# Twelve of the 832 edge steps get their node rows from SyncE, one register-addressed transfer a row, in place of GpSimd's gather

## The chip, the cores and the metric

One core of a Trainium2 chip runs the whole program. The metric is the device time of one execution in microseconds (us), as the median of several; lower is better. TensorE (PE), VectorE (DVE), ScalarE (ACT), GpSimd (POOL) and SyncE (SP) each run a program of their own and meet at semaphores. "Landed" is said of a DMA transfer when its completion has been signalled.

## The reference

A graph attention layer and a mixture of experts follow each other, each with a layer normalisation ahead and a residual around it. This change lies in the attention layer:

```python
N = 6250; E = 100000; H, F_IN, F_OUT = (8, 256, 32)
src, dst = (edge_index[0], edge_index[1])
h = jnp.einsum('ni,hio->hno', x, W)
attn_src = jnp.einsum('hno,ho->hn', h, a_src[..., 0])
attn_dst = jnp.einsum('hno,ho->hn', h, a_dst[..., 0])
edge_attn = jax.nn.leaky_relu(attn_src[:, src] + attn_dst[:, dst], negative_slope=0.2)
edge_attn_exp = jnp.exp(edge_attn - jnp.max(edge_attn))
attn_sum = jax.ops.segment_sum(edge_attn_exp.T, dst, num_segments=N)
attn_norm = edge_attn_exp / (attn_sum[dst].T + 1e-10)
out = jax.ops.segment_sum((attn_norm[..., None] * h[:, src]).transpose(1, 0, 2), dst, num_segments=N)
```

After it come a top-2 choice among 16 experts and two matrix products per expert (256 to 512 to 256), which the change does not touch.

## The kernel before, in words

The first stage normalises x, multiplies it by the weights and stores one row of 264 numbers a node (256 features, 8 attention terms; 1056 bytes) in the DRAM table `node_rows`. The edges are sorted by destination. They are cut into chunks of 128, and a chunk that crosses a border between two tiles of 128 destination nodes is worked once for each tile; that makes at most 832 steps (`STEPS`), in 104 groups of 8 (`GROUP`). The edge stage runs over the groups:

- GpSimd (`gpsimd_program`, L827) issues one indirect gather a step: 128 rows of `node_rows`, by the 128 indices of a column of `src_idx`, into `gathered[g % 4][:, j, :]`. There are four slots of eight steps. Before every second gather it waits until the matmuls of the same steps four groups earlier are done (`agg_mm`), since they read the slot.
- SyncE (`load_dloc`, L504) loads one broadcast block of local destination numbers a group, three groups ahead. It waits for the one-hot of three groups earlier (`onehot_t_ok`, from L1367). Between two of these it has nothing else to do.
- VectorE goes through a group in a fixed order, here called its turn. It sums the destination's terms (L1374), waits for the group's eight gathers and adds the sources' terms (`edge_logits_add`, L1381), then the leaky ReLU (L1386) and the maximum (L1392, L1397, L1399). Between nine or so adds of finished sums into the accumulator (`add_step`, L1419 and L1421) stand the one-hot of the next group (L1367) and four products of rows and weights (`weigh`, L1407), each over two steps. It reads the accumulator's tile numbers into registers with a register load (L444).
- ScalarE takes the running maximum (L688), writes the exponentials into the gathered rows (L693) and into PSUM (L695), and makes the one-hots for the sums.
- TensorE multiplies one-hots by weighed rows (`aggregate`, L973), two groups behind: the sums of group g - 2 stand in turn g. In the last eight turns (`CATCH_UP`) it has nine steps a turn, so that the last group is not two behind.

In the experts' stage SyncE loads an expert's first matrix for each of 113 slots, by an expert number that it reads into a register eight at a time (`experts_of`, L460) and uses as the offset of a transfer (L587). Lines are those of the kernel before.

Of the kernel before, what the change touches and what calls it, by code (L numbers as in the profile page):

```python
# [7 lines left out]
ACT = mybir.ActivationFunctionType  # L8
AXIS_FREE = mybir.AxisListType.X
F32 = mybir.dt.float32  # L10
I32 = mybir.dt.int32
# [30 lines left out]
SLOT_TILES = (NODES * TOP_K + EXPERTS * (P - 1)) // P  # L42
PAIRS = -(-TILES // 2)
Y_ROW = F_IN + TOP_K
KC = F_IN // P
# [5 lines left out]
def build_program(nc, x, src, dst, w_gnn, a_src, a_dst, gate_w, gate_b, w1, b1, w2, b2, gamma, beta, out):  # L51
    ctx = ExitStack()
    with ctx:
# [17 lines left out]
        dloc_rows = dram("dloc_rows", [STEP_BLOCKS * P, P], BF16)  # L71
        chunk_rows = dram("chunk_rows", [2 * CHUNK_PARTS * CHUNK_COLS])


# [198 lines left out]

        row_in = [sem(f"row_in{i}") for i in range(4)]
        rows_b_ok, dloc_out = sem("rows_b_ok"), sem("dloc_out")
        dloc_in = [sem(f"dloc_in{i}") for i in range(3)]
# [102 lines left out]
        slot_at.append(region1[:, fourth:fourth + GROUP * ROW])  # L379
        gathered = [v.rearrange("p (j c) -> p j c", c=ROW) for v in slot_at]  # L380
        Z_BANKS, M_BANK, AGG_BANKS = (2, 3), 4, (0, 1, 5, 6, 7)
        AGG = len(AGG_BANKS)
# [83 lines left out]
        def sync_program(d):  # L466
# [39 lines left out]
            for t in range(TILES):  # L506
# [16 lines left out]
                if t in ROWS_AT:  # L523
                    n = ROWS_AT.index(t)
                    d.wait_ge(rows_b_ok, n + 1)
                    d.dma_start(dloc_rows[n * P:(n + 1) * P, :], rows_b[:, n, :]).then_inc(dloc_out, 16)
            store_h(TILES - 1)
            d.wait_ge(dloc_out, 16 * STEP_BLOCKS)
            for g in range(3):
                load_dloc(g)  # L530


            for g in range(3, GROUPS):
                load_dloc(g)

            def store_y0(q):
# [78 lines left out]
        def scalar_program(s):  # L615
# [70 lines left out]
            for g in range(GROUPS):  # L686
                s.wait_ge(max_bc, g + 1)
                s.activation(neg_max[:, g + 1:g + 2], bank[M_BANK][:, P + 8:P + 9], ACT.Copy,  # L688
                             scale=-1.0).then_inc(neg_max_ok)
                s.wait_ge(neg_max_ok, g + 1)  # L690
                s.wait_ge(z_relu, g + 1)

                s.activation(gathered[g % SLOTS][:, :, F_IN:ROW], z[:, g % 2, :, :], ACT.Exp,  # L693
                             bias=neg_max[:, g + 1:g + 2])
                s.activation(p_bank(g), z[:, g % 2, :, :], ACT.Exp, bias=neg_max[:, g + 1:g + 2]).then_inc(p_ok)  # L695
                s.activation(fall[:, g:g + 1], neg_max[:, g:g + 1], ACT.Exp, scale=-1.0,
                             bias=neg_max[:, g + 1:g + 2]).then_inc(fall_ok)
                onehots(g)
                if g % 2 == 1 and g // 2 < TILES:
                    x_plus_xn(g // 2)  # L700
# [81 lines left out]
        def gpsimd_program(p):  # L782
# [32 lines left out]
            for g in range(GROUPS):  # L815
# [5 lines left out]
                if g == SLOTS - 1:  # L821
                    p.wait_ge(b1_col_ok, 1)
                for j in range(GROUP):
                    k = g * GROUP + j
# [71 lines left out]
        def tensor_program(pe):  # L896
# [69 lines left out]
            def aggregate(steps):  # L966
                for k in steps:
# [3 lines left out]
                    if k >= AGG:  # L971
                        pe.wait_ge(acc_add, k - AGG + 1)
                    pe.matmul(bank[AGG_BANKS[k % AGG]][:, 0:ROW], onehot[:, (g % 3) * GROUP + j, :],  # L973
                              gathered[g % SLOTS][:, j, :], start=True, stop=True).then_inc(agg_mm)
            pe.wait_ge(xnt_ok, TILES)
# [171 lines left out]
        def vector_program(v):  # L1147
# [229 lines left out]
            def edge_logits_add(g):  # L1377
                zg = z[:, g % 2, :, :]
                v.wait_ge(z_sum, g + 1)
                v.wait_ge(row_in[g % SLOTS], GROUP * landed(g, SLOTS))  # L1380
                v.tensor_tensor(zg, zg, gathered[g % SLOTS][:, :, F_IN:ROW], ALU.add).then_inc(z_add)  # L1381

# [19 lines left out]
            def weigh(g, quarter):  # L1402
                v.wait_ge(p_ok, g + 1)
                js = slice(quarter * 2, quarter * 2 + 2)
                hv = gathered[g % SLOTS][:, js, 0:F_IN].rearrange("p j (h o) -> p j h o", o=F_OUT)
# [436 lines left out]
```

## Time and profile before

| what | us |
|---|---|
| time, median of 3 runs (lowest to highest) | 1995.41 (1995.39 to 1996.13) |
| the profiled execution, first to last instruction (its span) | 1782.4 |
| median minus span | 213.0 |
| first gather of the edge stage starts | 91.5 |
| last gather starts | 1132.6 |

The profile is of one further execution, and what it gives as that execution's own time is its span; the 213.0 us between the span and the median of the runs lie outside it. The edge stage takes 1041.1 us from the first gather's start to the last one's. Busy shares over the span are 80% for PE, 62% for its weight loads (they overlap), 66% for DVE, 43% for ACT and 68% for POOL.

### The profile page before, as it was taken

How to read it: one execution, taken by the hardware profiler on the slowest of the kernel's cores; microseconds unless marked ns; L12 is line 12 of the kernel's file. 1: busy time of each engine (PE TensorE's matmuls, PEld its weight loads, DVE VectorE, ACT ScalarE, POOL GpSimd, SP SyncE). 2: the span in 40 equal slices, each digit the busy share in tenths (PEclk: the TensorE clock that was granted, in tenths of full speed). 3: DMA queues.
4: the chain of work that ended last, by engine and by line, in shares of the span. 5: the costliest groups of instructions: out<-in, count | busy, mean ns of one | idle time of the engine just before them, and what ended most of it. 6: DMA issues, size and time to landing. Idle time of an engine off the chain costs nothing.

```text
span 1782.4 us, 28293 instructions
## 1 busy us (share of the span) xinstructions
PE 1417.7 (80%) x6757; PEld 1097.9 (62%) x6757; DVE 1173.9 (66%) x3565; ACT 775.1 (43%) x2345; POOL 1206.3 (68%) x1237
## 2 busy tenths in 40 slices
PE   4937877777777878778777877667699999999965
PEld 3725555545555555455554555466599999999953
DVE  6767777777777777777777777799734443332348
ACT  2634545455454545454454544444323333333335
POOL 3077777777777777777777777337457667656747
PEclk9957677777777776876777687855599999999987
DMA  6555555545554555554444445364579778878875
GB/s 199 182 143 132 138 134 137 134 133 137 134 137 133 139 132 138 133 134 137 132 139 132 139 131 142 100 213 148 143 213 223 212 207 218 212 201 212 212 182 184
DMA packets 166544, 284.22 MB, mean 159 GB/s; under 512 B 31743, under 2 KB 93268, under 8 KB 166228
## 3 DMA queue, kind: packets, MB, share of 16 engines
q0 software_dynamic: 62256, 143.99, 32.9%
q1 hardware_dynamic: 101764, 137.90, 25.7%
q8 instruction: 65, 1.06, 0.2%
q10 hardware_dynamic: 2368, 0.52, 0.2%
q14 instruction: 91, 0.75, 0.1%
HBM read 240.97 MB, written 42.16 MB: 159 GB/s over the span
## 4 chain that ended last, share of the span: by engine, by line
PE 41%; POOL 23%; DVE 14%; issue 11%; DMA 8%; DVEq 2%; ACT 0%; ACTq 0%; POOLq 0%; SPq 0%
POOL region L827 22%; PE bank L1104 11%; PE bank L1116 11%; PE bank L973 10%; DMA region<-node_rows,region 6%; DVE region L1421 3%; PE bank L962 2%; PE bank L906 2%; PE bank L1093 1%; DVEq L444 1%; DVE region L1367 1%; DVE region L1419 1%; DVE region L1804 1%; PE bank L1023 1%; DVE stats L1792 1%
## 5 line engine op out<-in xcount | busy, mean ns | idle before, releaser
L827 POOL DMA_INDIRECT region<-node_rows,region x832 | 788.9, 948 | 295.9 <-issue 227.9
L973 PE MATMUL bank<-region 128*128 128x264 f32 x1664 | 646.3, 543 | 0.2
L973 PEld LDWEIGHTS bank<-region 128*128 128x128 f32 x1664 | 421.9, 271 | 98.3 <-issue 6.3
L1421 DVE TENSOR_TENSOR region<-region,bank 128x264 f32 x728 | 309.7, 425 | 117.9 <-PE bank L973 61.1
L1407 DVE TENSOR_TENSOR region<-region,bank 128x512 f32<-128x512 f32 x416 | 282.1, 679 | 3.4 <-ACT bank L695 3.4
L678 ACT ACTIVATE region<-iota_row,region 128x128 f32<-128x128 f32 x832 | 262.5, 386 | 0.0
L754 ACT ACTIVATE region<-bank,b_col 128x128 f32<-128x128 f32 x452 | 128.8, 368 | 304.3 <-PE bank L1104 300.8
L887 POOL DMA_INDIRECT sum_rows<-region,row_u x113 | 179.4, 1587 | 104.9 <-DVE region L1775 40.6
L688 ACT ACTIVATE neg_max<-bank 128x1 f32<-128x1 f32 x104 | 17.8, 171 | 532.5 <-PE bank L998 532.5
L1104 PEld LDWEIGHTS bank<-region 128*128 128x128 f32 x1808 | 219.5, 192 | 6.3 <-DVE region L1732 0.5
L1104 PE MATMUL bank<-region 128*128 128x128 f32 x1808 | 220.2, 275 | 0.3 <-DVE region L1732 0.3
L1116 PE MATMUL bank<-region 128*128 x904 | 214.2, 380 | 0.1
L1116 PEld LDWEIGHTS bank<-region 128*128 128x128 f32 x904 | 162.9, 190 | 18.5 <-issue 1.0
L683 ACT ACTIVATE region<-region,ones 128x512 f32<-128x512 f32 x208 | 150.2, 722 | 6.7
L1775 DVE SCALAR_TENSOR_TENSOR region<-bank,region 128x256 f32<-128x256 f32 x113 | 54.7, 484 | 142.0 <-PE bank L1116 75.2
L998 PE MATMUL bank<-run_max,ones 1*128 1x1 f32 x208 | 42.9, 273 | 131.7 <-DVE run_max L1399 131.7
L860 POOL DMA_INDIRECT region<-y_rows,token_u x113 | 112.0, 991 | 51.1 <-issue 25.6
L998 PEld LDWEIGHTS bank<-run_max,ones 1*128 1x128 f32 x208 | 34.0, 203 | 176.8 <-DVE run_max L1399 176.8
L1732 DVE COPY region<-bank 128x256 f32<-128x256 f32 x113 | 47.8, 423 | 118.4 <-PE bank L1093 118.4
L617 ACT ACTIVATE region<-bank 128x256 f32<-128x256 f32 (+4 forms) x182 | 63.7, 379 | 81.2 <-PE bank L1034 41.9
L962 PE MATMUL bank<-attn_parts,region 128*128 x832 | 95.3, 195 | 0.2
L1419 DVE SCALAR_TENSOR_TENSOR region<-region,fall,bank 128x264 f32 x104 | 50.8, 488 | 66.1 <-issue 40.4
(242 smaller groups left out, 1539.9 us busy)
## 6 DMA issues: line engine op xcount, KB each, us to landing
region<-in_L_ffn_w SPq DMA_DIRECT2D x129, 512.0 KB, 5.0
region<-dloc_rows SPq DMA_DIRECT2D x104, 256.0 KB, 3.5
region<-node_rows,region POOLq DMA_INDIRECT x832, 2.8
node_rows<-region SPq DMA_DIRECT2D x12, 528.0 KB, 3.4
y_rows<-region SPq DMA_DIRECT2D x7, 896.0 KB, 6.0
sum_rows<-region SPq DMA_DIRECT2D x7, 896.0 KB, 7.6
region<-in_x SPq DMA_DIRECT2D x5, 896.0 KB, 8.6
region<-sum_rows SPq DMA_DIRECT2D x5, 896.0 KB, 11.0
```

Source lines behind the costliest of these rows:

```text
L678: ins = s.activation(onehot[:, slot + j, :], iota_row[:, :], ACT.Square, bias=dloc[:, k:k + 1], scale=-1.0)
L683: s.activation(four, four, ACT.Relu, bias=ones[:, 0:1], scale=-1.0).then_inc(onehot_ok)
L754: ins = s.activation(hidt_buf[:, j % 2, f * P:(f + 1) * P], bank[HIDT_BANKS[j % 2]][:, f * P:(f + 1) * P], ACT.Relu, bias=flat_b1[:, bass. ...
L827: p.indirect_dma_start(gathered[g % SLOTS][:, j, :], None, node_rows, bass.IndirectOffsetOnAxis(src_idx[:, k:k + 1], 0)).then_inc(row_in[g ...
L860: p.indirect_dma_start(xg_buf[:, j % XG, :], None, y0_rows, bass.IndirectOffsetOnAxis(token_u[:, j:j + 1], 0)).then_inc(xg_in[j % XG], 16)
L887: p.indirect_dma_start(sum_rows, bass.IndirectOffsetOnAxis(row_u[:, j:j + 1], 0), y_buf[:, j % 3, :], None, compute_op=ALU.add).then_inc(y ...
L962: ins = pe.matmul(z_bank(g)[:, j * AD:(j + 1) * AD], onehot_t[:, g % 2, j, :], flat_parts[:, bass.ds(tiles[j] * AD, AD)], start=False, sto ...
L973: pe.matmul(bank[AGG_BANKS[k % AGG]][:, 0:ROW], onehot[:, (g % 3) * GROUP + j, :], gathered[g % SLOTS][:, j, :], start=True, stop=True).th ...
L1104: ins = pe.matmul(bank[HIDT_BANKS[j % 2]][:, f * P:(f + 1) * P], w1_buf[:, j % W1_SLOTS, c * HIDDEN + f * P:c * HIDDEN + (f + 1) * P], xgt ...
L1116: ins = pe.matmul(bank[Y_BANKS[j % 2]][:, 0:F_IN], hidt_buf[:, j % 2, f * P:(f + 1) * P], w2_sb[:, bass.ds(expert * (FC * F_IN) + f * F_IN ...
L1407: v.tensor_tensor(hv, hv, pv, ALU.mult).then_inc(weigh_ok)
L1421: v.tensor_tensor(rows, rows, new, ALU.add).then_inc(acc_add)
```

## The change

From group 9 on, the last step of every eighth group (9, 17, ..., 97) is no longer gathered by GpSimd. These are twelve steps; I call their groups side groups and their turns side turns. Here is what the diff does, engine by engine:

- **GpSimd** issues seven gathers in a side group, so 820 in all (the printed order has one row of x832 before and of x820 now).
- **SyncE** copies the twelve steps' source numbers in the first stage from the rows that were fetched for the tables to a small DRAM table (`side_src`), in twelve small transfers. In the edge stage, after each of the 96 `load_dloc` of groups 3 to 98, it reads 16 node numbers into registers with one register load and issues 16 transfers of one row each, from `node_rows` to one partition of a side buffer. Eight such turns fill one buffer of 128 rows. There are two buffers, by turns. Before the first part of step m it waits for the matmul of step m - 2 on the same buffer and loads the numbers of step m + 1 into an SBUF row.
- **VectorE** adds the logits of a side group in two pieces, seven steps and one, with a wait on the side transfers between them, and weighs its last two steps with two instructions in place of one.
- **ScalarE** writes the exponentials of a side group with two instructions in place of one.
- **TensorE** has the same matmuls; twelve of them read the side buffer.

```diff
+SIDE_PART = 16
+SIDE_TURNS = P // SIDE_PART
+SIDE_FIRST = SIDE_TURNS + 1
+SIDES = (GROUPS - 1 - SIDE_FIRST) // SIDE_TURNS + 1
...
+        def side_of(g):
+            m, rest = divmod(g - SIDE_FIRST, SIDE_TURNS)
+            return m if rest == 0 and 0 <= m < SIDES else None
...
+                    for m in range(SIDES):
+                        if side_step(m) // P == n:
+                            r = side_step(m) % P
+                            d.dma_start(side_src[m:m + 1, :], rows_i[r:r + 1, 2 * n, :]).then_inc(side_src_out, 16)
...
+            def side_rows(m, part):
+                if part == 0:
+                    if m >= 2:
+                        d.wait_ge(agg_mm, side_step(m - 2) + 1)
+                    if m + 1 < SIDES:
+                        load_side_idx(m + 1)
+                    d.wait_ge(side_idx_in[m % 2], landed(m, 2))
+                e0 = part * SIDE_PART
+                _, nodes = nc.values_load_multi_w_load_instructions(
+                    side_idx[0:1, m % 2, e0:e0 + SIDE_PART], engines=[d.engine], min_val=0, max_val=NODES - 1,
+                    skip_runtime_bounds_check_because="a node's number by the inputs' kind")
+                for i in range(SIDE_PART):
+                    d.dma_start(side[e0 + i:e0 + i + 1, m % 2, :], node_rows[bass.ds(nodes[i], 1), :]).then_inc(
+                        side_in[m % 2], 16)
+            d.wait_ge(side_src_out, 16 * SIDES)
+            load_side_idx(0)
+            for i in (H_OUTS - 2, H_OUTS - 1):
+                d.wait_ge(h_out[i % 2], landed(i, 2))
             for g in range(3, GROUPS):
                 load_dloc(g)
+                if g - 3 < SIDES * SIDE_TURNS:
+                    side_rows((g - 3) // SIDE_TURNS, (g - 3) % SIDE_TURNS)
...
-                s.activation(gathered[g % SLOTS][:, :, F_IN:ROW], z[:, g % 2, :, :], ACT.Exp,
+                n = gathers_of(g)
+                s.activation(gathered[g % SLOTS][:, 0:n, F_IN:ROW], z[:, g % 2, 0:n, :], ACT.Exp,
                              bias=neg_max[:, g + 1:g + 2])
+                if n < GROUP:
+                    s.activation(row_of(g, n)[:, F_IN:ROW], z[:, g % 2, n, :], ACT.Exp, bias=neg_max[:, g + 1:g + 2])
...
-                for j in range(GROUP):
+                for j in range(gathers_of(g)):
...
-                v.wait_ge(row_in[g % SLOTS], GROUP * landed(g, SLOTS))
-                v.tensor_tensor(zg, zg, gathered[g % SLOTS][:, :, F_IN:ROW], ALU.add).then_inc(z_add)
+                v.wait_ge(row_in[g % SLOTS], row_landed(g))
+                n = gathers_of(g)
+                ins = v.tensor_tensor(zg[:, 0:n, :], zg[:, 0:n, :], gathered[g % SLOTS][:, 0:n, F_IN:ROW], ALU.add)
+                if n < GROUP:
+                    v.wait_ge(side_in[side_of(g) % 2], side_landed(side_of(g)))
+                    ins = v.tensor_tensor(zg[:, n, :], zg[:, n, :], row_of(g, n)[:, F_IN:ROW], ALU.add)
+                ins.then_inc(z_add)
...
+                if quarter == 3 and side_of(g) is not None:
+                    for j in range(GROUP - 2, GROUP):
+                        hv = row_of(g, j)[:, 0:F_IN].rearrange("p (h o) -> p h o", o=F_OUT)
+                        ins = v.tensor_tensor(hv, hv, p_bank(g)[:, j, :].unsqueeze(2).broadcast_to([P, HEADS, F_OUT]),
+                                              ALU.mult)
```

SyncE's program at the start of the edge stage, before. The row with x104 is all of `load_dloc`; behind it comes what follows the edge stage:

```order
L499 DMA node_rows<-region 128x4x264 x3
L499 DMA node_rows<-region 128x264
L504 DMA region<-dloc_rows 128x1024 x104
L548 DMA sum_rows<-ones 768x1x128
L552 DMA region<-in_L_ffn_b 128x4096
```

The same place now (L537 is `load_dloc`, L571 `load_side_idx`, L581 the register load, and ISA the register arithmetic ahead of a row's transfer at L585):

```order
L532 DMA node_rows<-region 128x4x264 x3
L532 DMA node_rows<-region 128x264
L537 DMA region<-dloc_rows 128x1024 x3
L571 DMA region<-side_src 1x128
L537 DMA region<-dloc_rows 128x1024
L571 DMA region<-side_src 1x128
L581 TENSOR_LOAD region
L585 ISA
L585 DMA region<-node_rows 1x264
```

The last two rows stand 16 times in a turn, so that 96 pieces of one register load, 16 register operations and 16 transfers have come between `load_dloc`'s transfers.

VectorE's program in the turn of group 9, before, at its start and at its end:

```order
L1374 TENSOR_REDUCE z<-bank 128x64
L1381 TENSOR_TENSOR z<-z,region 128x64
L1386 SCALAR_TENSOR_TENSOR z<-z 128x64
...
L1421 TENSOR_TENSOR region<-region,bank 128x264
L1407 TENSOR_TENSOR region<-region,bank 128x2x256
```

The same rows now:

```order
L1437 TENSOR_REDUCE z<-bank 128x64
L1445 TENSOR_TENSOR z<-z,region 128x56
L1448 TENSOR_TENSOR z<-z,region 128x8
L1454 SCALAR_TENSOR_TENSOR z<-z 128x64
...
L1496 TENSOR_TENSOR region<-region,bank 128x264
L1475 TENSOR_TENSOR region<-region,bank 128x256 x2
```

One add has become two, and the last product over two steps has become two over one step each. The other 92 turns read as before.

## Rows read from the trace of the kernel before

**Rows 1.** The page: span, and shares of the chain that ended last.

```profile
span 1782.4 us, 28293 instructions
...
POOL region L827 22%; PE bank L1104 11%; PE bank L1116 11%; PE bank L973 10%; DMA region<-node_rows,region 6%; DVE region L1421 3%; PE bank L962 2%; PE bank L906 2%; PE bank L1093 1%; DVEq L444 1%; DVE region L1367 1%; DVE region L1419 1%; DVE region L1804 1%; PE bank L1023 1%; DVE stats L1792 1%
```

**Rows 2.** Busy time by stretch, two halves of the edge stage's steady part.

```profile
core 0: us, PE busy (x) PEld busy (x) DVE busy (x) ACT busy (x) POOL busy (x), PEclk, DMA share, GB/s
130.00:600.00 470.00, 361.84 (x1315) 244.23 (x1314) 348.84 (x894) 233.48 (x682) 355.78 (x376) 0.76 0.50 135
600.00:1070.00 470.00, 367.50 (x1310) 249.03 (x1309) 348.50 (x893) 232.56 (x679) 355.58 (x376) 0.74 0.50 135
```

**Rows 3.** The gathers' line: durations (ns), idle time ahead, time to landing.

```profile
L827 POOL DMA_INDIRECT region<-node_rows,region x832: 942/946/1910, 91.5 to 1132.6; - x167
...
  issue: 227.9, 748
...
DMA to landing us min/median/max: 2.7/2.8/4.5
```

**Rows 4.** GpSimd in order of time: start, length, idle time ahead.

```profile
601.68 0.95 POOL L827 DMA_INDIRECT region<-node_rows,region  x1 [0.30 <-issue]
602.93 0.95 POOL L827 DMA_INDIRECT region<-node_rows,region  x1 [0.30 <-PE bank L973]
```

**Rows 5.** TensorE in order of time, the sums at the turn's border.

```profile
590.29 4.59 PE L973 MATMUL bank<-region 128*128 128x264 f32 x12
```

**Rows 6.** Groups of instructions, 130 to 1070 us: count, busy us, mean ns, idle ahead.

```profile
L1421 DVE TENSOR_TENSOR region<-region,bank 128x264 f32 x658 | 279.9, 425 | 98.7 <-PE bank L973 54.0 <-DVE region L1421 19.9 <-DVE region L1419 17.5
L1407 DVE TENSOR_TENSOR region<-region,bank 128x512 f32<-128x512 f32 x375 | 254.7, 679 | 0.0
...
L1381 DVE TENSOR_TENSOR z<-z,region 128x64 f32<-128x64 f32 x94 | 21.2, 226 | 70.8 <-DMA region<-node_rows,region 70.6
...
L688 ACT ACTIVATE neg_max<-bank 128x1 f32<-128x1 f32 x94 | 16.1, 171 | 464.7 <-PE bank L998 464.7
```

**Rows 7.** VectorE in order of time: two waits for gathered rows.

```profile
375.45 0.23 DVE L1381 TENSOR_TENSOR z<-z,region 128x64 f32<-128x64 f32 x1 [1.55 <-DMA region<-node_rows,region]
...
1075.59 0.23 DVE L1381 TENSOR_TENSOR z<-z,region 128x64 f32<-128x64 f32 x1 [0.29 <-DMA region<-node_rows,region]
```

**Rows 8.** The groups view of the last turns, 1086 to 1139 us.

```profile
L1381 DVE TENSOR_TENSOR z<-z,region 128x64 f32<-128x64 f32 x6 | 1.4, 225 | 0.2
```

**Rows 9.** SyncE's waits: who for whom, total us, times, longest.

```profile
SPq L504 <- DVE region L1367: 979.8, 101, 12.3
...
SPq L499 <- ACT region L617: 43.6, 12, 10.1
```

**Rows 10.** `load_dloc` between 139 and 1062 us: durations (ns), first and last start.

```profile
L504 SPq DMA_DIRECT2D region<-dloc_rows x93: 319/320/320, 140.0 to 1060.1; - x93
```

**Rows 11.** SyncE's register-addressed transfers: durations, and the first two in time.

```profile
L587 SPq DMA_DIRECT2D region<-in_L_ffn_w x113: 372/373/403, 1286.2 to 1700.0; - x113
...
1286.23 0.97 SPq L587 DMA_DIRECT2D region<-in_L_ffn_w  x2
```

**Rows 12.** Register loads: SyncE's line, and VectorE's between 1070 and 1139 us.

```profile
L460 SPq TENSOR_LOAD <-expert_row x15: 288/527/916, 1285.3 to 1696.6; - x15
...
L444 DVEq TENSOR_LOAD <-tile_row x13: 306/321/1872, 1073.5 to 1136.6; - x13
```

**Rows 13.** SyncE's transfers of one partition or row, in order of time.

```profile
1.68 0.28 SPq L478 DMA_DIRECT2D region<-in_dst  x1
2.00 0.37 SPq L480 DMA_DIRECT2D region<-in_dst  x1
2.42 0.30 SPq L482 DMA_DIRECT2D region<-in_dst  x1
...
4.50 0.43 SPq L490 DMA_DIRECT2D src_pad<-region  x1
4.97 0.24 SPq L491 DMA_DIRECT2D dst_pad<-region  x1
```

More of the change, by code:

```diff
@@ L72, in build_program @@
         chunk_rows = dram("chunk_rows", [2 * CHUNK_PARTS * CHUNK_COLS])
+        side_src = dram("side_src", [SIDES, P], I32)
         region0 = sb("region0", [P, TILES * F_IN + 2 * BATCH * F_IN])
@@ L274, in build_program @@
         row_in = [sem(f"row_in{i}") for i in range(4)]
+        side_in = [sem(f"side_in{i}") for i in range(2)]
+        side_src_out, side_idx_in = sem("side_src_out"), [sem(f"side_idx_in{i}") for i in range(2)]
         rows_b_ok, dloc_out = sem("rows_b_ok"), sem("dloc_out")
@@ L380, in build_program, with side_step, side_landed, gathers_of @@
         gathered = [v.rearrange("p (j c) -> p j c", c=ROW) for v in slot_at]
+        side = region2[:, (SLOTS - 1) * GROUP * ROW:(SLOTS - 1) * GROUP * ROW + 2 * ROW].rearrange(
+            "p (r c) -> p r c", r=2)
+        side_idx = region1[0:1, fourth + GROUP * ROW:fourth + GROUP * ROW + 2 * P].rearrange(
+            "a (r m) -> a r m", r=2).bitcast(I32)
+        assert fourth + GROUP * ROW + 2 * P <= EXPERTS * FC * F_IN
+        def side_of(g):
+            m, rest = divmod(g - SIDE_FIRST, SIDE_TURNS)
+            return m if rest == 0 and 0 <= m < SIDES else None
+        def side_step(m):
+            return (SIDE_FIRST + m * SIDE_TURNS) * GROUP + GROUP - 1
+        def side_landed(m):
+            return 16 * P * (m // 2 + 1)
+        def gathers_of(g):
+            return GROUP if side_of(g) is None else GROUP - 1
+        def row_landed(g):
+            return 16 * sum(gathers_of(i) for i in range(g % SLOTS, g + 1, SLOTS))
+        def row_of(g, j):
+            if j == GROUP - 1 and side_of(g) is not None:
+                return side[:, side_of(g) % 2, :]
+            return gathered[g % SLOTS][:, j, :]
         Z_BANKS, M_BANK, AGG_BANKS = (2, 3), 4, (0, 1, 5, 6, 7)
@@ L530, in sync_program, with load_side_idx @@
                 load_dloc(g)
+            def load_side_idx(m):
+                d.dma_start(side_idx[:, m % 2, :], side_src[m:m + 1, :]).then_inc(side_idx_in[m % 2], 16)
+            def side_rows(m, part):
[16 more added lines that the diff above has]
+                d.wait_ge(h_out[i % 2], landed(i, 2))
             for g in range(3, GROUPS):
                 load_dloc(g)
+                if g - 3 < SIDES * SIDE_TURNS:
+                    side_rows((g - 3) // SIDE_TURNS, (g - 3) % SIDE_TURNS)
             def store_y0(q):
@@ L973, in aggregate @@
                     pe.matmul(bank[AGG_BANKS[k % AGG]][:, 0:ROW], onehot[:, (g % 3) * GROUP + j, :],
-                              gathered[g % SLOTS][:, j, :], start=True, stop=True).then_inc(agg_mm)
+                              row_of(g, j), start=True, stop=True).then_inc(agg_mm)
             pe.wait_ge(xnt_ok, TILES)
@@ L1403, in weigh @@
                 v.wait_ge(p_ok, g + 1)
+                if quarter == 3 and side_of(g) is not None:
[3 more added lines that the diff above has]
+                                              ALU.mult)
+                    ins.then_inc(weigh_ok)
+                    return
                 js = slice(quarter * 2, quarter * 2 + 2)
```

## The prediction

> **What bounds the kernel now.** I read the page's chain first, then the stretches of the edge stage, then what ended each engine's waits there. In the chain the gathers (L827) are the largest single line, 22% of the span, and their landing is another 6% [rows 1]; in the rest of the kernel nothing is touched, so only the edge stage counts. In its steady part no compute engine is full: of 470 us PE is busy 362 to 368, DVE 349, POOL 356, and the DMA engines half of the time [rows 2]. POOL's 356 hides that it never waits for anyone. A gather takes 0.946 us, and the idle time ahead of it is 0.30 us (227.9/748) [rows 3], also where the wait for the sums of four groups before is named as what ended it; two neighbours start 1.25 us apart [rows 4]. So a group of eight costs POOL 10.0 us, and (1132.6 - 91.5)/831 = 1.253 us is the mean pitch over the whole stage [rows 3]. What idles is DVE: in 94 turns it waited 70.6 us for the gathered rows, 0.75 us a turn [rows 6]. Its own loop is therefore 10.0 - 0.75 = 9.25 us long, and POOL's issue sets the pace with a margin of only 0.75 us a turn.
>
> Two more things must be seen. POOL has room to run ahead: the gather at 602.93 is the first of its group and needs the first two sums of four groups before, which lie in the block of matmuls that ends at 590.29 + 4.59 = 594.88 [rows 4, 5], so 8.0 us earlier. And at the very end POOL is not the bound: before 1075.59 (group 97) DVE still waited 0.29 us [rows 7], in the six turns from 1086 to 1139 us only 0.2 us in all [rows 8]. Those turns carry nine sums in place of eight and run at DVE's and PE's own pace.
>
> **What it saves.** Twelve gathers at 1.25 us are 15.0 us of POOL. Eleven of them lie in groups 9 to 89: 13.75 us. DVE takes a gain of 1.25 us over two or three turns (0.75 a turn), and has eight until the next, so it is whole again each time: eight groups cost POOL 78.75 us and DVE 8 x 9.25 = 74.0 plus the extra work below. The twelfth, in group 97, meets a DVE that had 0.29 us to wait: it gives 0.29, and the last 1.0 us is lost, because the turns behind it are not POOL's. Sum: 14.04 us.
>
> **What it adds to a side turn.** A second add in front of the ReLU: 0.23 us (the one over eight steps takes 0.226 [rows 6]; bounds 0.1 and 0.26 with a gap). A second exponential on ScalarE ahead of the one into PSUM that DVE waits for: 0.20 us, between nothing and 0.4, nearest the small L688 (0.171 [rows 6]) and a gap. Two products over one step in place of one over two: 2 x 0.425 (L1421, nearly the same shape) - 0.679 = 0.17 us [rows 6]. Together 0.6 us. In eleven side turns DVE's spare 0.75 a turn covers it: 74.0 + 0.6 is below 78.75. In turn 97 it is on the path: -0.6 us. Without that cover it would be 12 x 0.6 = 7.2 us.
>
> **What it adds to SyncE.** This decides the case. Between two `load_dloc` SP waits 979.8/101 = 9.70 us [rows 9]; the cadence falls by 1.25/8 = 0.16, which leaves 9.54 us a turn for one register load and 16 rows. The register load: eight numbers take 0.527, the shortest (one number) 0.288 [rows 12]. If the price goes by number, 16 take 0.80; if by pieces of four (two pieces 0.53, one 0.29), 0.29 + 3 x 0.24 = 1.0. I take 1.0 and 0.03 for a gap. A row: the first two register-addressed transfers of L587 span 0.97 us, of which the transfers themselves are 2 x 0.39; so the register operations and gaps between are 0.19 us [rows 11]. The transfer instruction itself, with one row, is not in the trace with a register; five static ones of one partition took 0.24, 0.28, 0.30, 0.37 and 0.43 [rows 13], the 128-partition ones 0.32 [rows 10] and 0.37 [rows 11]. I take the middle one, 0.30 (the 0.32 is close by), and keep 0.24 and 0.43 as ends. Then 1.03 + 16 x 0.49 = 8.9 us, with ends 0.83 + 16 x 0.43 = 7.7 and 1.03 + 16 x 0.62 = 11.0. 8.9 fits into 9.54: `load_dloc` is issued when it was, and a side buffer is complete about two turns before its group needs it. With that, SP adds nothing; the first buffer starts at about 101 us and has six turns. The twelve small copies, 12 x 0.30 = 3.6 us if nothing covered them, stand among stores before which SP waits 43.6 us for ACT in all [rows 9]: nothing.
>
> The rows' bytes are the same as the gathers' that they replace, and the DMA engines are half busy [rows 2]; a later landing shifts the whole stage once and does not change the pace. Landings already scatter: 1.55 us of waiting at 375.45 against 0.75 in the mean [rows 6, 7]. I take 0 and keep 1.3 us as the bad end.
>
> Sum on the profiled execution: 14.04 - 0.6 = 13.4 us, span 1782.4 to 1769.0. What lies outside the span, 213.0 us, I leave as it is (the trace does not show it); 1995.4 - 13.4 = **1982.0 us**, 0.7% faster. 4 us (0.2%) is about what a measurement tells from no change.
>
> The Trainium skill speaks against the idea as a whole: "DMA: Bandwidth & Descriptors", section "Issuing engines are not separate DMA queues", says that all issuers share the same 16 DMA engines and that another issuer saves only the sequencer's time to start a transfer, which it calls usually small. By that rule the gain would be about nothing, 1995.4. The gathers' rows say that starting the transfer is just what is bound here, 1.25 us of POOL a gather beside DMA engines at 0.50, so the sum by the rows stands.
>
> **The rivals.**
>
> *SyncE becomes the bound (slower).* If a turn of SP takes longer than the cadence, it falls behind in every one of 96 turns. With T for the whole turn (`load_dloc` 0.36 and the rest), turns from the fifth on start at 140.0 [rows 10], 92 are left, and a row lands about 3 us after its issue (gathers 2.8 [rows 3]): group 97 cannot start before 143 + 92 T. It should start at 1075.6 - 14.0 = 1061.6, which is T = 9.98, or 0.35 us a transfer instruction. At T = 10.14 (0.36) group 97 starts when it did before. With L587's 0.373 T is 1.39 + 16 x 0.563 = 10.4 and group 97 starts at 1100: +24, +0.6, 2020 us; with 0.43 T is 11.3, about 2105. A second way there: register loads of eight took up to 1.87 us [rows 12], those whose first number lies off a multiple of four; 16 such numbers would take some 3.7 and T be 11.9. SP's loads start at multiples of 16, so I give that little. For it: two of five one-row prices are above 0.35, and the margin is 0.05 us. Against: both stand near the start of the kernel, one beside ACT's issues and one behind a semaphore wait, and the repeat of each is shorter. Chance 0.16; half of it beyond 2000.
>
> *SP just at the edge.* T between 9.98 and 10.14 gives part of the gain: 1983 to 1996. Chance 0.05.
>
> *The gain is swallowed by DVE's loop (no change, or little).* Its margin is 0.75 us a turn. If the landings came later and scattered more, since a side transfer is one small packet among the gathers', and SP's longer program is fetched by DMA too, this would matter only above (78.75 - 74.0 - 0.6)/8 = 0.5 us a turn, which is all that is left of DVE's margin. 1990 to 1995. Chance 0.05.
>
> The same page, section "Why a DMA increments its semaphore by 16 and not by 1", says that a one-partition transfer from SP goes through one DMA engine, the lowest-numbered. By that rule all 1536 rows queue on a single engine that already has its share of every gather. In a mechanism of this kernel: one engine's busy share rises from 0.50 [rows 2] by 16 packets a turn; only if a packet cost 0.3 us would it pass 0.98 and set the pace, and every group would then take 10 us or more: 1996 or above. Chance 0.03; no row here shows a one-row transfer's packets.
>
> *The forecast*: chance 0.71. Its own range is 1980.4 (all 15.0 us arrive) to 1984.5 (landings 1.3 us later, and extras of 1.7 in turn 97).
>
> **How the numbers follow.** Faster (below 1991.4): the forecast 0.71, 0.04 of the edge cases and 0.02 of DVE's, 0.77. Slower (above 1999.4): SP's bound 0.16 and 0.01 of the single engine's, 0.17. The rest, 0.06, is no change. For 8 in 10 the range takes the forecast's own, and the edge and DVE cases (together 0.81): 1980.3 to 1995.
>
> **What would show it.** Right: 820 gathers still 1.25 us apart with 0.30 ahead of each; group 97's logits start near 1061.6; DVE's wait ahead of its first add falls from 0.75 to about 0.5 a turn and is near nothing in the turn behind a side group; no wait of DVE for the side transfers; SP still waits for L1367 every turn, about 0.6 us. Wrong: SP's waits for L1367 vanish, `load_dloc` is issued later and later, and DVE waits ahead of the second add in side turns; or POOL's idle time before a gather grows beyond 0.30 for sums of four groups before.

## The result, and the profile after

| | kernel before | changed kernel | ratio (95% interval) |
|---|---|---|---|
| recorded measurement, median us | 1995.77 (4 runs) | 2215.96 (4 runs, 2211.55 to 2220.68) | 1.1103 (1.1089 to 1.1117) |
| the same two kernels on a later occasion | 1784.25 (7 runs) | 1770.48 (4 runs) | 0.9931 (0.9911 to 0.9951) |

The change made the kernel 220 us slower where it was measured, and 14 us faster on a later occasion. The measurements fall into two kinds, with nothing between: on occasions of **kind A** the kernel before takes 1981 to 1996 us, on occasions of **kind B** 1783 to 1784 us (medians). The runs' time is 1.8 to 1.9 us more than the span in either kind (1981.39 and 1979.5 us for one execution of the kernel before), so nothing like 213 us lies outside the span. The profile of before in the rows ahead of the prediction (span 1782.4) is of kind B, the times beside it are of kind A. Experiments are compared with the kernel before of their own occasion only. Their recorded expectations speak of chips of one kind or the other; but chip number 4 stands beside an occasion of kind B and, 26 minutes later, beside one of kind A, so the kind does not go with that number.

The groups view (line, engine, operation, count | busy us, mean ns | idle ahead, and what ended it) of VectorE's instructions in the changed kernel, kind A, 110 to 1490 us:

```profile
L1496 DVE TENSOR_TENSOR region<-region,bank 128x264 f32 x665 | 283.1, 426 | 233.6 <-PE bank L1036 168.7 <-issue 32.7 <-remote 16.0
...
L1430 DVE TENSOR_SCALAR region<-region,iota_col 128x1024 bf16<-128x1024 bf16 x97 | 47.5, 490 | 144.0 <-DMA region<-dloc_rows 142.0 <-issue 1.9
```

VectorE no longer waits for gathered rows (5.7 us ahead of L1445 in this stretch, against 70.8 in [rows 6]). It waits for what SyncE sends: 142.0 us for `load_dloc` ahead of L1430, and for the side rows ahead of L1448, as the view of line L585 says (first the durations in ns, min/median/max, then who waited):

```profile
L585 SPq FUSED_REGOPS  x1536: 1/37/1405, 111.6 to 1489.3; - x192
L585 SPq MOVE region<-node_rows x1536: 1/29/1404, 111.7 to 1489.4; - x192
L585 SPq DMA_DIRECT2D region<-node_rows x1536: 1/228/1424, 111.7 to 1489.5; - x192
...
  DVE z L1448: 140.9, 12
```

From the first register load at 110.3 us to the last at 1481.6 SyncE has 95 turns of 14.4 us, and between the last row's transfer of a turn and the next `load_dloc` lie 0.05 us (median of 96 turns): it no longer waits. (Its waits for VectorE, 979.8 us in [rows 9], are gone from the waits view but for one, but that view proves nothing in kind A, as the next section shows.) SyncE is the bound, and every engine does less in the same time than in [rows 2] (the busy time by stretch):

```profile
core 0: us, PE busy (x) PEld busy (x) DVE busy (x) ACT busy (x) POOL busy (x), PEclk, DMA share, GB/s
110.00:600.00 490.00, 281.19 (x941) 181.53 (x940) 249.26 (x647) 170.96 (x498) 265.41 (x279) 0.64 0.36 97
600.00:1100.00 500.00, 290.68 (x1010) 186.26 (x1009) 267.62 (x693) 179.61 (x526) 271.26 (x286) 0.68 0.37 97
```

279 gathers in 490 us where [rows 2] has 376 in 470. How SyncE came to be late, its timeline shows: seven rows took 9.19 us at one place, and three took 1.09 a little later.

```profile
509.12 9.19 SPq L585 DMA_DIRECT2D region<-node_rows  x7
518.36 0.36 SPq L537 DMA_DIRECT2D region<-dloc_rows  x1
520.11 1.09 SPq L585 DMA_DIRECT2D region<-node_rows  x3
```

The medians (37, 29, 228 ns) are short, so it is not the price of a row that is high; some instructions are stretched, up to 1.4 us, and it meets register operations and transfers alike. I call the time from one instruction's start to the next one's a step. Between the fourth and the hundredth `load_dloc`, with the register loads left out, 856 of 4716 steps of SyncE's program last over 0.56 us (mostly about 0.7), and they make 782 of 1275 us; of those that begin with a register operation or move it is 0.17, of those that begin with a transfer 0.21. The other engines' programs are not stretched alike: from 130 to 960 us the 464 register operations of VectorE last at most 69 ns, TensorE's 472 at most 46; only a few of VectorE's 59 register loads, mostly 0.60 us, reach up to 0.85.

### The profile page after: what moved, and what is told of

Its sections match the earlier page's. It is cut to its first block and busy times, and to the rows that moved or that the text cites. A ratio compares the mean times of both kernels' runs of the same rounds, so it can differ in the third digit from the quotient of the medians.

```text
span 2215.4 us, 33047 instructions
## 1 busy us (share of the span) xinstructions
PE 1468.4 (66%) x6757; PEld 1106.9 (50%) x6757; DVE 1173.5 (53%) x3589; ACT 778.1 (35%) x2357; POOL 1201.5 (54%) x1225
## 5 line engine op out<-in xcount | busy, mean ns | idle before, releaser
L1036 PE MATMUL bank<-region 128*128 128x264 f32 x1664 | 690.1, 566 | 45.9 <-DVE region L1496 33.8
L1482 DVE TENSOR_TENSOR region<-region,bank 128x512 f32<-128x512 f32 x404 | 273.9, 679 | 36.2 <-issue 23.4
L1055 PE MATMUL bank<-ident,zmax 128*1 128x128 f32 x104 | 32.3, 310 | 268.7 <-DVE zmax L1460 213.3
L1055 PEld LDWEIGHTS bank<-ident,zmax 128*1 128x1 f32 x104 | 8.5, 82 | 308.3 <-DVE zmax L1460 237.0
L1022 PE MATMUL bank<-far_row,ones_b 1*128 1x256 bf16 x104 | 37.5, 361 | 174.5 <-DVE region L1430 137.8
L1061 PE MATMUL bank<-run_max,ones 1*128 1x1 f32 x208 | 51.2, 313 | 136.4 <-DVE run_max L1467 58.9
L1061 PEld LDWEIGHTS bank<-run_max,ones 1*128 1x128 f32 x208 | 42.3, 252 | 190.3 <-issue 106.7
L1022 PEld LDWEIGHTS bank<-far_row,ones_b 1*128 1x128 bf16 x104 | 10.1, 97 | 234.5 <-DVE region L1430 169.7
```

The lines of the kernel that those rows point to most:

```text
L1061: pe.matmul(bank[M_BANK][:, P + 8:P + 9], ones[0:1, :], run_max[:, g + 1:g + 2], start=True, stop=True).then_inc(max_bc)
L1482: v.tensor_tensor(hv, hv, pv, ALU.mult).then_inc(weigh_ok)
```

## The experiments

**The kernel before, profiled again.** No edit.

> The kernel before, unchanged, for its profile beside its time: in the changed kernel time and span differ by 1.8 us, in the profile of before by 213. If the 213 us lie outside the program, the span is again 1782 and the time 1995. If the profiled execution of before was unlike the timed ones, the span is near 1993, and the gathers' pitch or DVE's waits show where the 211 us lie (1.50 us a gather in place of 1.25 would do).

1981.39 us, kind A (13 runs of the kernel before on this occasion: median 1981.45). Its busy time by stretch, and the gathers' view:

```profile
core 0: us, PE busy (x) PEld busy (x) DVE busy (x) ACT busy (x) POOL busy (x), PEclk, DMA share, GB/s
110.00:600.00 490.00, 343.63 (x1133) 220.13 (x1133) 295.62 (x765) 204.77 (x595) 323.75 (x337) 0.66 0.43 116
```

```profile
L827 POOL DMA_INDIRECT region<-node_rows,region x832: 940/947/2313, 100.5 to 1311.4; - x167
...
  issue: 219.5, 719
  PE bank L973: 180.3, 109
...
  DVE z L1381: 4.3, 2
```

Against [rows 3] a gather is as long (947 ns), but the mean pitch is (1311.4 - 100.5)/831 = 1.457 us and not 1.253: GpSimd now waits 180.3 us for sums of four groups before, and VectorE hardly waits for rows (4.3 us in all, against 79.3 in the same view of the profile of kind B). A turn is 11.7 us. VectorE waits for TensorE instead (waits, 130 to 1200 us):

```profile
DVE region L1421 <- PE bank L973: 265.7, 91, 3.1
```

The timeline of one turn, VectorE and then TensorE, shows a wait that TensorE's work does not account for:

```profile
610.24 0.43 DVE L1421 TENSOR_TENSOR region<-region,bank 128x264 f32 x1 [3.06 <-PE bank L973]
```

```profile
606.48 5.45 PE L973 MATMUL bank<-region 128*128 128x264 f32 x12
```

The twelve matmuls of the block start about 0.44 us apart from 606.48 on (their ends are modelled, their starts are not), so the first sums were done before 608; the trace's records of the signals that they count up stand at 610.11, 610.16, 610.21 and 610.36, in a bunch. In kind A the bound seems to be the loop of VectorE and TensorE with such late signals; this is read from one turn and from the sum of the waits, and no run took the lateness away by itself. The granted clock is 0.66 against 0.76 of full speed [rows 2] in this stretch, that is, TensorE spends more of it at its lower level, 1.2 GHz; it stands idle more in each turn, and I cannot tell what of it is cause and what effect.

The waits view must be read with care in kind A. SyncE's transfer of `load_dloc` takes 0.32 us in each turn of 11.7, and SyncE has nothing else to do, but the view gives it

```profile
SPq L504 <- DVE region L1367: 60.7, 5, 25.7
```

five waits in place of 101: about half of the semaphore records are missing, as told at the end. A wait that the view does not name in kind A may be there all the same. What SyncE had left in a turn is therefore taken from the starts of its instructions below.

**Transfers from fixed addresses.** The sixteen transfers of a turn stay, without register loads and register arithmetic (the loads' values are not used any more, and the trace has none). The rows are other nodes', so the output is not the reference's.

```diff
-                    d.dma_start(side[e0 + i:e0 + i + 1, m % 2, :], node_rows[bass.ds(nodes[i], 1), :]).then_inc(
+                    d.dma_start(side[e0 + i:e0 + i + 1, m % 2, :], node_rows[e0 + i:e0 + i + 1, :]).then_inc(
```

> The row transfers take rows of fixed addresses, so that a turn of SyncE has 18 instructions in place of 50, with the same 16 transfers (the side rows are then other nodes' rows). Theory instructions (each instruction of SyncE's pays the 0.7 us steps seen in the trace): the lost time falls to about a third, a turn to about 9 us, under the cadence, and the time is near before. Theory transfers (16 one-row transfers a turn are too much for the path behind SyncE): turns stay near 14 us, the time at 2150 to 2216.

1980.1 us against 1981.45, ratio 0.9993 (0.9984 to 1.0003), kind A. SyncE keeps up: from a `load_dloc` to the turn's last row it is at work 6.8 us (median), and 5.0 us are left. Twelve gathers fewer bring nothing: GpSimd is not the bound in kind A.

**Half the rate.** Eight rows a turn, six gathers removed.

```diff
-SIDE_PART = 16
+SIDE_PART = 8
```

> Eight rows a turn in place of sixteen, so that six steps and not twelve are fetched by SyncE. Both theories: the loss per turn is at most halved, a turn is 7 to 8 us and under the cadence, SyncE waits for DVE again and the time is 1995 less some 7 us. If it stays far above 1995, the loss does not come from SyncE's rate.

1990.64 us, ratio 1.0043 (1.0026 to 1.0059), kind A; again on another occasion of kind A:

> The changed kernel with eight rows a turn in place of sixteen, so that six gathers are removed and not twelve. Where the kernel before took 1981 us it took 1990.6 us. On a chip where the kernel before takes 1783 us, SyncE's turn is about 0.4 + 0.6 + 8 x 0.41 = 4.3 us and hidden: if each removed gather is worth 1.15 us, as the twelve removed ones were (13.8 us), the time is 1783.5 - 6.9 = 1776.6 us; if something else gave the 13.8 us, 1783 or 1770 us. I expect 1776.6 us.

1989.30 us against 1981.18, ratio 1.0040 (1.0027 to 1.0054). So the loss is not in proportion to the rows (8 us for half, 220 for all), as for a queue that starts to count when it is longer than the turn: here SyncE is at work 7.5 us of a turn of 11.8. VectorE waits for no transfer of SyncE's in these two; where the 8 us come from I did not find. What half the rate gives in kind B (1776.6 was expected) was not measured.

**Rows that nobody reads.** All 832 gathers as before, SyncE's work as changed.

```diff
-            m, rest = divmod(g - SIDE_FIRST, SIDE_TURNS)
-            return m if rest == 0 and 0 <= m < SIDES else None
+            return None
```

> All 832 steps are gathered and worked as before; SyncE issues its 1536 row transfers all the same, and nobody reads them (the output is the reference's). Theory late load_dloc: SyncE's turn of 14.8 us alone sets the pace through the destination numbers, 2200 or more. Theory late rows (the stage only waits for the side buffers): 1995, or a little over.

2218.57 us, ratio 1.1188 (1.1150 to 1.1226), kind A: the whole loss, with neither second add nor side rows awaited. It comes through `load_dloc`, which stands behind the rows in SyncE's program (groups view, 110 to 1500 us):

```profile
L1431 DVE TENSOR_SCALAR region<-region,iota_col 128x1024 bf16<-128x1024 bf16 x99 | 49.3, 498 | 335.2 <-DMA region<-dloc_rows 313.8 <-issue 21.3
```

**Waits in place of rows.** As the unread run, with 96 waits a turn whose values were reached long before.

```diff
+                for i in range(6 * SIDE_PART):
+                    d.wait_ge(dloc_out, 16 * (1 + i % STEP_BLOCKS))
```

> All 832 gathers stay, the register loads and the row transfers are left out, and in their place SyncE runs 96 waits a turn whose values were reached long ago. If SyncE is slowed at any instruction (after the change about one step in five of SyncE was some 0.7 us long, whatever the instruction), 96 short instructions cost 96 x (0.03 + 0.2 x 0.7) = 16 us a turn, more than the 11.65 us of a turn of the kernel before in these runs: the time is about 1981 + 96 x 4.7 = 2430 us, and waits of some 0.7 us stand in SyncE's rows. If only instructions that hand out a transfer or touch a register are slowed, the 96 waits cost some 3 us a turn and the time is 1981 us. The output is that of the kernel before.

1784.02 us, ratio 1.0006 (0.9996 to 1.0015), kind B; a second time kind B again (1784.0, ratio 1.0005). Whether plain waits are stretched in kind A stays open.

**The removed gathers alone.** One transfer of 128 neighbouring rows fills a side buffer (other nodes' rows, so the output is not the reference's).

```diff
+                if part == 7:
+                    d.dma_start(side[:, m % 2, :], node_rows[m * P:(m + 1) * P, :]).then_inc(side_in[m % 2], 16)
```

> The changed kernel with its 820 gathers, but each side buffer is filled by one transfer of 128 neighbouring rows, without register loads and one-row transfers (the rows are other nodes', so the output is not the reference's). It measures the removed gathers alone. By the prediction's step on the pace of GpSimd they are worth 13 to 14 us (1968 us against 1981); by what the run with transfers from fixed addresses showed, nothing: 1981 us within 2 us.

1770.63 us against 1783.10, ratio 0.9928 (0.9911 to 0.9944), kind B. Here the gathers are the bound, and twelve fewer bring 12.5 us. In kind A this edit was not measured.

**The changed kernel again.** No edit.

> The changed kernel, unchanged, on whichever chip it falls to; the kernel before has so far taken 1995.8 us and 1981.5 us on two occasions and 1783.1 us on a third, where SyncE's rows and register loads (beside one-hots left out) went at 8.2 us a turn and cost nothing. If the prediction's account holds where the kernel before takes about 1783 us, the changed one is faster there by 12 to 13 us (as the block transfers were), about 1771 us, with SyncE waiting in every turn. If this falls where the kernel before takes about 1980 us or more, the changed kernel takes 2200 to 2220 us again.

1770.48 us against 1784.25, kind B: 13.8 us faster. The chain that ended last is the one of [rows 1] again, the gathers at its head:

```profile
span 1767.4 us, 33047 instructions
...
POOL region L890 21%; PE bank L1167 11%; PE bank L1179 11%; PE bank L1036 9%; DMA region<-node_rows,region 5%; DVE region L1496 3%; PE bank L1025 2%; PE bank L969 2%; DVEq L477 1%; PE bank L1156 1%; DVE region L1494 1%; DVE region L1430 1%; DVE region L1879 1%; PE bank L1086 1%; DVE stats L1867 1%
```

And by stretch, for [rows 2]:

```profile
130.00:600.00 470.00, 367.10 (x1333) 249.14 (x1331) 353.52 (x920) 236.76 (x694) 355.76 (x376) 0.76 0.51 138
600.00:1040.00 440.00, 339.76 (x1252) 232.33 (x1252) 331.39 (x859) 223.77 (x655) 332.77 (x353) 0.78 0.51 138
```

As many gathers in the same time (376), and 1333 matmuls in place of 1315: the turn is shorter by the gathers left out. SyncE's instructions are as short as they are in the medians of kind A, but none is stretched:

```profile
L585 SPq FUSED_REGOPS  x1536: 37/37/51, 101.2 to 1042.4; - x192
L585 SPq MOVE region<-node_rows x1536: 29/29/38, 101.3 to 1042.4; - x192
L585 SPq DMA_DIRECT2D region<-node_rows x1536: 224/228/308, 101.3 to 1042.5; - x192
```

**More rows.** As the unread run, with eight more one-row transfers a turn, from `node_rows` to a DRAM table.

```diff
+                for i in range(8):
+                    d.dma_start(side_more[m * SIDE_TURNS + part:m * SIDE_TURNS + part + 1, i, :],
+                                node_rows[bass.ds(nodes[i], 1), :]).then_inc(side_in[m % 2], 16)
```

> The unread run (832 gathers, 16 register-addressed rows a turn that nobody reads) with eight more one-row transfers a turn, 24 in all. On a chip where the kernel before takes 1783 us and SyncE is undisturbed, its turn is 0.40 + 1.20 + 24 x 0.41 = 11.5 us against the 10.0 us that the stage gives it: if SyncE's turn becomes the stage's pace once it is the longer, the time is 1783 + 96 x 1.5 = 1927 us; if SyncE's ring of three buffers hides it, 1783 us. I expect 1927 us. On a chip where the kernel before takes about 1980 us, the turn grows from 14.4 us by some 6 us, to about 2750 us.

2274.67 us, ratio 1.2747 (1.2726 to 1.2768), kind B, where 1927 was expected. I had priced the eight at 0.41 us each. They go to DRAM, and cost much more:

```profile
L588 SPq DMA_DIRECT2D side_more<-node_rows x768: 700/729/1459, 108.1 to 1574.1; - x192
```

From the fourth to the hundredth `load_dloc` SyncE's turn is 15.37 us in the trace, and VectorE waits 508.6 us for `load_dloc`'s transfers between 130 and 1500 us. My price was wrong, the mechanism right: on the undisturbed kind too, a SyncE turn longer than the stage's turn becomes the stage's turn. By the prediction's own formula 15.37 gives 143 + 92 x 15.37 = 1557 us for group 97 and a time of 1783.6 + (1557 - 1075.6) = 2265 us.

**Few gathers.** As the unread run, but gathers are issued for the first four groups alone and later groups read those rows again (the output is not the reference's).

```diff
+                    if g >= SLOTS:
+                        continue
...
-                v.wait_ge(row_in[g % SLOTS], row_landed(g))
+                v.wait_ge(row_in[g % SLOTS], row_landed(g % SLOTS))
```

> The changed kernel's row transfers and register loads stay, unread, with all 832 steps' gathers in the code, but the gathers are issued for the first four groups alone and later groups read those rows again, so the output is not the reference's. If the gathers' packets are what slows SyncE, its turns fall to about the 8.2 us that the undisturbed turns of the changed kernel took, SyncE waits for VectorE again, and the time is that of the kernel before or less (1981 us at most). If ScalarE's work alone does it, SyncE stays at about 14 us a turn and the time near 2200 us. By the shares of slow instructions seen so far (0.18 with ScalarE busy and no gather moving, 0.58 with both) I expect a turn of 9 to 11 us.

1700.1 us against 1783.1 in kind B (three occasions: 1700.1, 1701.0, 1700.0). A fourth occasion was of kind A:

> Gathers for the first four groups only, rows and register loads unread (the output is not the reference's). On a chip where the kernel before takes 1783 us: 1700 us, as before. On a chip where it takes about 1980 us: if the gathers' packets are what slows SyncE, its turns fall to 8 to 9 us and the time to 1700 to 1850 us; if ScalarE's instructions alone do it, 14 us a turn and about 2200 us. I expect the first.

1727.71 us against 1981.18, ratio 0.8721 (0.8705 to 0.8737), two executions. This is the run that tells. SyncE has the same rows and register loads as in the unread run, which was 14.5 us a turn in kind A; here its turn is 9.2 us, as long as VectorE's loop, and 17 of 3072 register steps last over 0.56 us, where it was 546 of 3072. On the line of the rows the longest register operation is 0.7 us, not 1.4:

```profile
L584 SPq FUSED_REGOPS  x1536: 3/37/711, 110.3 to 992.8; - x192
L584 SPq MOVE region<-node_rows x1536: 3/29/699, 110.4 to 992.9; - x192
```

VectorE's waits for TensorE shrank with it, to the size that they have in this kernel in kind B (39.6 us there, 130 to 970 us; the row here is 130 to 990):

```profile
L1499 DVE TENSOR_TENSOR region<-region,bank 128x264 f32 x651 | 277.6, 426 | 85.1 <-PE bank L1039 40.3 <-DVE region L1499 19.7 <-DVE region L1497 15.6
```

So both marks of kind A, the stretched instructions of SyncE and the late signals of TensorE, need the gathers. Of the 17 stretched register steps 10 begin while a packet of the few gathers is moving, which is true of 17 register steps in all; of the other 3055 seven are stretched. ScalarE's activations go on in this run: 1348 register steps begin beside one, and 5 of them are stretched. What of a gather does it, GpSimd's instruction, the packets or the semaphore updates that come with them, the run does not separate, since it leaves out all three.

**Few one-hots.** As the unread run, without ScalarE's one-hots from the fourth group on (in each half of a group two very short activations stand for five; the output is not the reference's).

```diff
+                    if g >= 3:
+                        s.wait_ge(onehot_ok, 2 * g + half)
+                        s.activation(small[:, 5:6], ones[:, 0:1], ACT.Copy).then_inc(onehot_sq)
+                        s.wait_ge(onehot_sq, 2 * g + half + 1)
+                        s.activation(small[:, 5:6], ones[:, 0:1], ACT.Copy).then_inc(onehot_ok)
+                        continue
```

> As the unread run, with all 832 gathers, but ScalarE's one-hots are left out from the fourth group on (two very short activations stand in for ten), so the output is not the reference's. If ScalarE's activations are what slows SyncE, its turns fall towards 8.2 to 10 us and the time to 1981 us or less; if the gathers' packets are, SyncE stays near 14 us a turn and the time near 2200 us. By the shares seen (0.26 with gathers alone, 0.58 with both) I expect about 10 to 11 us a turn.

1786.37 us, ratio 1.0026 (1.0014 to 1.0038), kind B; two more tries fell to kind B as well (1787.3 and 1786.3). It tells nothing of kind A. In the changed kernel's trace of kind A the stretched share of the 3072 register steps was 0.55 of those that begin beside both a gather's packet and an activation, 0.22 beside a packet alone, 0.23 beside an activation alone and 0.05 beside neither (other ways to count moved the shares by some hundredths, that beside an activation alone by more). The third share did not outlive the gathers (5 of 1348 in the run above), so activations do not do it by themselves. Whether they add to what the gathers do was not measured in kind A.

## Why the prediction was wrong

**The step that failed is the one on SyncE's turn, "8.9 fits into 9.54".** Its undisturbed size was too high, not too low. Nine rows stand in one row of the later profile's timeline (kind B):

```profile
509.16 3.52 SPq L585 DMA_DIRECT2D region<-node_rows  x9
```

That is (3.52 - 0.23)/8 = 0.41 us a row, where I took 0.49: the transfer 0.228 (taken: 0.30, with 0.24 as the lower end, so the bounds missed it too), register work and gaps 0.18 (taken: 0.19). The register load of 16 took 1.165 (taken: 1.0). From a `load_dloc` to the last row SyncE is at work 8.2 us (median, 8.35 in the mean). It waits for VectorE again:

```profile
SPq L537 <- DVE region L1430: 183.6, 98, 10.8
```

These waits hold the last turns too, which have no rows; in the 96 turns with rows 1.5 us of 9.85 are left, where 0.6 was forecast. In the recorded measurement the same instructions took 14.4 us a turn, because nearly every fifth step was stretched (856 of 4716), and the stage's own turn there was 11.7 us and not 9.54. The prediction had only prices of instructions that stood alone in a calm trace; it had no term for what gathers in flight do to SyncE, and its rival "SyncE becomes the bound", with the right mechanism and a chance of 0.16, looked for the cause in a row's price. What stretches them is open, see below.

**"What lies outside the span, 213.0 us, I leave as it is" was wrong too.** Only 1.8 to 1.9 us lie outside. The difference of 213 us between the time and the profiled span was the mark of kind A, and most of it lay in the stage that the change touches. Between the spans 1782.4 and 1979.5 us lie 197 us: 170 from the first gather to the last (1210.9 against 1041.1 us, a turn being 11.7 us against 10.0), 9 ahead of it (first gather 100.5 against 91.5 us) and 18 behind it. The first occasion was 14 us slower than this one of kind A, for a reason not found. A span 11% below the times shown says that the profile is not of the executions that are timed; a sum made in it may not be carried over.

**"POOL's issue sets the pace"**: true of kind B (block_side, 12.5 us), false of kind A (rows_static, nothing).

**What it saves and adds (14.04 and 0.6, together 13.4 us)**: measured 13.8 us in kind B, for the reasons given. The total of 1982.0 us mixed this with a time of kind A; neither kind gave it. The gathers' and VectorE's lines of the changed kernel there:

```profile
L890 POOL DMA_INDIRECT region<-node_rows,region x820: 942/946/2245, 89.6 to 1116.0; - x164
...
  issue: 216.9, 712
...
  DVE z L1445: 68.7, 72
```

820 gathers, (1116.0 - 89.6)/819 = 1.253 us apart, 0.30 ahead of each (216.9/712), as forecast. Group 97's side add starts at 1059.73 us, forecast 1061.6 for its logits:

```profile
1059.60 0.22 DVE L1445 TENSOR_TENSOR z<-z,region 128x56 f32<-128x56 f32 x1
1059.73 0.16 DVE L1448 TENSOR_TENSOR z<-z,region 128x8 f32<-128x8 f32 x1
```

It has no wait ahead of it, as forecast; VectorE's wait for gathered rows fell to 55.9 us in 88 turns (130 to 1000 us; 0.64 a turn, forecast 0.5). The added instructions took 0.17 (second add, taken 0.23), 0.28 (exponential, taken 0.20) and 2 x 0.412 - 0.679 = 0.15 us (taken 0.17).

**SyncE as the bound, T = 14.4.** In kind A the stage had 11.7 us a turn, so the loss is (14.38 - 11.73) x 96 = 254 us over the turns with rows; The spans differ by 2215.4 - 1979.5 = 236 us: some 18 us are won back behind these turns, since from the hundredth `load_dloc` to the last gather it is 57 us where the kernel before has 76. The recorded medians differ by 220, the earlier occasion's kernel before being 14 us slower than this one. The unread run confirms that `load_dloc` in the queue behind the rows is enough for the whole loss.

**The rivals by a rule.** The Trainium skill, "DMA: Bandwidth & Descriptors", section "Issuing engines are not separate DMA queues", made the gain about nothing: so it was in kind A without the register work (0.9993), not in kind B (0.9931). The single DMA engine was no bound: the traces have one packet of 1056 bytes for each of the 1536 rows (7808 such packets in the changed kernel, 6272 before), and 16 rows a turn from fixed addresses cost nothing in kind A.

**What stretches the instructions, and what stays open.** The gathers' packets themselves are no slower in kind A: 167.4 ns a packet in the mean against 167.7 (130 to 1000 us, kernel before). What differs is what was written down. The traces of kind B give a time from `load_dloc`'s issue to its landing (3.5 us for the kernel before), those of kind A give none; of the kernel before the trace holds 28868 records of counted-up semaphores in kind B and 14769 in kind A, of the few-gathers kernel 19227 and 16259; instruction records are complete in both (28293 for the kernel before). It is not the number of records alone: the run with more rows has 40299 in kind B, and no register step of it is stretched. The issues' view of the kernel before, kind A, 130 to 1200 us, ends each row without the time to landing:

```profile
region<-dloc_rows SPq DMA_DIRECT2D x90, 256.0 KB
region<-node_rows,region POOLq DMA_INDIRECT x733
```

The Trainium skill, "NOTIFIC — the notification-queue block", section "Overflow: three behaviours, one of which stalls the engine", describes the block that writes the records of engines and semaphores to rings in memory: its internal pipeline holds the producer back rather than lose a record, and a full ring drops new records, unless it is set to overwrite old ones or to stall the producer. That would fit held-back instructions and lost semaphore records where gathers' records come in numbers. But this is argued, not shown: no run here was made without records, none counts the block's stalls, and why an occasion is of one kind or the other is not known. It cannot be told from this case what the two kernels take with nothing recorded.

No version was found that is faster in both kinds: the changed kernel gains 0.7% in one and loses 11% in the other, at half the rate it loses 0.4% in kind A, and kind B was not measured.

## What to carry to other kernels

Compare the profiled execution's span with the times shown before anything else: if they differ by more than a few us, the profile may be of a kernel with another bound, and a gain read from it may not be there. Many short instructions on an engine whose next instruction is awaited every turn are safe only with much spare time, more than their calm prices say (here 8.2 us of work in 11.7 us was not enough). Issuing the awaited transfer turns ahead does not help once the queue's turn is the longer one: `load_dloc` runs three groups ahead here, and the lateness added up over 96 turns. To put it on another queue than the many short instructions would be the thing to try; no run here did. What such a move can win (here twelve gathers of 832) is small against what a late queue costs, which is its whole lateness.

## What the hardware showed unexpectedly

- The same kernel has two spans, 1782.4 and 1979.5 us, on one core. With SyncE's rows added, unread, and the gathers from the fifth group on left out they are 1698.1 and 1724.8 us: most of what tells the two kinds apart goes with the gathers.
- In a trace of kind A (changed kernel) 517 of SyncE's 3072 register steps are stretched to over 0.56 us, in one of kind B none; VectorE's and TensorE's register operations last at most 69 and 46 ns in the former too.
- On SyncE, undisturbed, a one-row transfer with a register's address takes 0.228 us to a partition and 0.41 us with its register work; the same row to DRAM takes 0.729 us.
- A register load of 16 numbers takes SyncE 1.165 us, against 0.527 for eight [rows 12]: 0.08 us for each further number.
